# Cross-attention on one core: row sums by a transposing VectorE pass, a turned slot order, and variances from ScalarE

## The reference

```python
Q, K, V = split_heads(x @ Wq + bq), split_heads(ctx @ Wk + bk), split_heads(ctx @ Wv + bv)
scores = einsum('bhqd,bhkd->bhqk', Q, K) / sqrt(32)
attn = softmax(scores, axis=-1)                      # over 77 keys
out = merge_heads(einsum('bhqk,bhkd->bhqd', attn, V)) @ Wo + bo
y = out + x
mu, var = mean(y), mean(square(y - mu))              # over the 512 features
result = (y - mu) * rsqrt(var + 1e-5) * gamma + beta
```

## Time and profile before

| | |
|---|---|
| median of 3 runs | 676.41 us (676.19 to 676.54) |
| the profiled execution | 677.69 us, its span 675.9 us |
| mean granted TensorE clock | 0.983 |
| busy TensorE, VectorE, GpSimd, ScalarE | 643.8, 555.0, 453.7, 319.7 us |
| chain of waits, by engine | TensorE 77%, VectorE 6%, SP's queue 6% |

### The profile page before, as it was taken

How to read it: one execution, slowest core, us unless ns; L and a number is a source line. 1 busy time by engine, 2 the same in 40 slices (tenths; PEclk the granted TensorE clock), 3 DMA queues, 4 the chain that set the end, 5 groups by cost and what they waited for, 6 DMA issues and landing times.

```text
span 675.9 us, 11503 instructions
## 1 busy us (share of the span) xinstructions
PE 643.8 (95%) x3336; PEld 435.1 (64%) x3336; DVE 555.0 (82%) x842; ACT 319.7 (47%) x547; POOL 453.7 (67%) x396
## 2 busy tenths in 40 slices
PE   6989997999999999999999999999999999999990
PEld 5978754666666666666666666666666666665570
DVE  5534484888889898888988888889888888988986
ACT  5612254545545555554555545455554544544431
POOL 0422143477777777777787777777877777666897
PEclk9999996999999999999999999999999999999996
DMA  9757788767776868778787778686767778675512
GB/s 318 288 198 186 193 203 208 179 162 199 194 201 170 209 180 205 204 195 215 201 197 184 201 186 204 190 201 186 198 177 206 198 205 215 152 185 154 162 62 93
DMA packets 105677, 129.55 MB, mean 192 GB/s; under 512 B 49936, under 2 KB 49936, under 8 KB 105648
## 3 DMA queue, kind: packets, MB, share of 16 engines
q1 hardware_dynamic: 105648, 129.19, 71.8%
HBM read 53.94 MB, written 24.35 MB: 116 GB/s over the span
## 4 chain that ended last, share of the span: by engine, by line
PE 77%; DVE 6%; SPq 6%; issue 2%; POOL 1%; DMA 1%; ACT 0%; POOLq 0%; DVEq 0%; ACTq 0%
PE p_q L584 24%; PE p_o L646 23%; PE p_s L614 9%; PE p_v L627 9%; PE p_d L630 7%; PE p_a L600 5%; SPq L519 3%; DVE rden L799 2%; SPq L505 1%; DMA xt<-in_x_t 1%; DVE cxt L813 1%; DVE stats L795 1%; DVE y L793 0%; POOL rstd L932 0%; DVE stats L887 0%
## 5 line engine op out<-in xcount | busy, mean ns | idle before, releaser
L799 DVE RECIPROCAL rden<-p_d 128x512 f32<-128x512 f32 x64 | 214.9, 3358 | 27.8 <-PE p_d L630 27.7
L709 ACT ACTIVATE prob<-p_s 77x512 f32<-77x512 f32 x256 | 144.0, 588 | 111.4 <-PE p_s L614 111.0
L834 DVE TENSOR_REDUCE nm<-p_a 128x4 f32<-128x308 f32 x256 | 117.4, 462 | 29.3 <-PE p_a L600 26.0
L936 POOL TENSOR_TENSOR y<-y,gamma_row 128x512 f32<-128x512 f32 x60 | 76.7, 1278 | 70.7 <-ACT y L739 70.7
L926 POOL TENSOR_TENSOR xl<-xt,xh 128x512 fp32r<-128x512 f32 x60 | 77.5, 1291 | 64.8 <-ACT xh L716 63.5
L584 PE MATMUL p_q<-xh,wqh 128*128 128x512 f32 x256 | 101.8, 398 | 1.7 <-PEq L148 1.7
L584 PE MATMUL p_q<-xl,wqh 128*128 128x512 f32 x256 | 101.8, 398 | 0.0
L584 PE MATMUL p_q<-xh,wql 128*128 128x512 f32 x256 | 101.1, 395 | 0.0
L945 POOL TENSOR_TENSOR cl<-cxt,ch 128x512 fp32r<-128x512 f32 x64 | 82.5, 1288 | 26.3 <-ACT ch L734 26.3
L739 ACT ACTIVATE y<-y,nmr,rstd 128x512 f32<-128x512 f32 x60 | 48.9, 815 | 106.1 <-DVE nmr L818 106.1
L614 PE MATMUL p_s<-z,ks 97*77 97x512 f32 x256 | 95.7, 414 | 0.0
(11 more groups left out here) (114 smaller groups left out, 911.8 us busy)
## 6 DMA issues: line engine op xcount, KB each, us to landing
z<-qh SPq DMA_DIRECT2D x256, 128.0 KB, 2.7
xt<-in_x_t SPq DMA_DIRECT2D x64, 256.0 KB, 2.8
z<-ql SPq DMA_DIRECT2D x128, 128.0 KB, 2.4
xn<-in_x SPq DMA_DIRECT2D x60, 256.0 KB, 3.1
out_dram<-y SPq DMA_DIRECT2D x60, 256.0 KB, 3.3
ks<-k_high SPq DMA_DIRECT2D x32, 154.0 KB, 3.5
cx<-in_ctx_t SPq DMA_DIRECT2D x4, 616.0 KB, 5.4
k_high<-kth SPq DMA_DIRECT2D x4, 616.0 KB, 3.5
```

Source lines behind the costliest of these rows:

```text
L709: nc.scalar.activation(prob[0:S2, j, :], p_s[j % 2][0:S2, :], ACT.Exp, scale=SCALE).then_inc(prob_ready, 1)
L799: nc.vector.reciprocal(rden[:], p_d[:]).then_inc(rden_ready, 1)
L834: nc.vector.tensor_reduce(nm[:, t, HC * (g.k % 2):HC * (g.k % 2 + 1)], p_a[t % 2][:, 0:HC * S2].rearrange("p (h k) -> p h k", k=S2), AX_X, ...
```

## The change: what it does

The sums over keys are formed in two steps. VectorE's new `sum_keys` reduces `prob` (96 partitions, rows from 64 on zeroed once at the start and then written as far as 77) with a transposing `tensor_reduce`: each block of 32 x 32 is turned and summed, which leaves `part`, 96 x 64. TensorE adds the three blocks of 32 with a 0/1 matrix `sel` into 16 columns per head (`p_den`); `invert_sums` takes the reciprocal of 16 columns and spreads it to `rden` with a transposition.

`add_residual` now yields the row sums as well (`accum_out`); a small operation makes the negated mean, ScalarE's new `square` yields the sum of squared deviations (its elementwise output goes to `xn`, unused), and `variance_of_squares` replaces `bn_stats` and `bn_aggr` for all but the last four tiles.

The slots are turned: maxima in the chunk's own slot, scores at + 2, values at + 3, out projection at + 7, norm at + 8, store at + 10. TensorE's slot begins with all of p_q. SP issues the z copies in the odd slot of the pair itself and the maxima in the next slot. The program has 67 slots instead of 69. The V products that are left to `attend` move up (`V_SLOTS`), and so does the loading of `Wo` (`WO_SLOTS`).

```diff
+KP = 3 * DK
...
-LAG_ROWMAX = 1
-LAG_PV = 5
-LAG_SCORE = 4
-LAG_OUT = 9
-LAG_NORM = 10
-LAG_SCALE = 11
-LAG_STORE = 12
+LAG_SCORE = 2
+LAG_PV = 3
+LAG_OUT = 7
+LAG_NORM = 8
+LAG_SCALE = 9
+LAG_STORE = 10
+WO_SLOTS = (3, 5)
 
 V_FIRST = 4
-V_SLOTS = (0, 1, 1, 2, 3, 3)
+V_SLOTS = (0, 0, 1, 1, 2, 2)
...
-                nc.gpsimd.memset(keep["ones"][:], 1.0)
                 nc.gpsimd.memset(keep["minus_half"][:], -0.5)
+                sel = keep["sel"]
+                nc.gpsimd.memset(sel[:], 0.0).then_inc(sel_ready, 1)
+                for b in range(KP // DK):
+                    pool.wait_ge(sel_ready, b + 1)
+                    nc.gpsimd.affine_select(out=sel[:], in_=sel[:], compare_op=ALU.not_equal, fill=1.0, base=-DK * b,
+                                            pattern=[[-1, DK]], channel_multiplier=1).then_inc(sel_ready, 1)
...
             def slot(g):
-                if g.k % 2 == 1 and g.back(3).valid(NG):
-                    load_maxima(g.back(3))
                 if g.k % 2 == 0 and g.back(2).valid(NG):
-
-
-                    c = g.back(2)
+                    load_maxima(g.back(2))
+                if g.k % 2 == 1 and g.back(1).valid(NG):
+
+
+                    c = g.back(1)
                     i = c.k // 2 % 2
                     all_at_least(sp, (qh_ready, c.over(1, 2)), (ql_ready, c.over(1, 2)),
                                  (s_summed, c.over(2, -1, HALF)))
@@ -518,14 +530,14 @@
                         for j in range(HC):
                             sp.dma_start(z[DK * part:DK * (part + 1), i, j::HC, :].bitcast(F32),
                                          src[DK * j:DK * (j + 1), i, :, :].bitcast(F32)).then_inc(z_in[i], 16)
-                if g.k % NCH == 1 and g.valid(NG):
-                    load_ks(g.back(1))
-                if g.k % NCH == 3 and g.valid(NG):
-                    load_v(g.back(3))
-                if g.k % NCH == NCH - 1 and g.back(-1).valid(NG):
-                    if g.back(NCH - 1).is_first():
+                if g.k % NCH == 0 and g.valid(NG):
+                    load_ks(g)
+                if g.k % NCH == 2 and g.valid(NG):
+                    load_v(g.back(2))
+                if g.k % NCH == 1 and g.back(1 - NCH).valid(NG):
+                    if g.back(1).is_first():
                         sp.wait_ge(kb1_zeroed, 1)
-                    load_kb(g.back(-1))
+                    load_kb(g.back(1 - NCH))
...
-                    all_at_least(sp, (y_ready, m.over(1, -1)))
+                    all_at_least(sp, (squared, m.over(1, -1)))
                     sp.dma_start(xn[:, m.k % 2, :], x_dram[m.over(1)]).then_inc(xn_in[m.k % 2], 16)
...
+                pe.wait_ge(part_ready, g.over(1, 1))
+                at_least(pe, rec_ready, g.over(1))
                 for j in range(HC):
-                    last = nc.tensor.matmul(p_d[DK * j:DK * (j + 1), :], ones[0:S2, :], prob[0:S2, j, :],
+                    last = nc.tensor.matmul(p_den[DK * j:DK * (j + 1), 0:QB], sel[:], part[:, QB * j:QB * (j + 1)],
                                             start=True, stop=True)
...
-                q, r, s, v, o = g, g.back(LAG_ROWMAX), g.back(LAG_SCORE), g.back(LAG_PV), g.back(LAG_OUT)
+                s, v, o = g.back(LAG_SCORE), g.back(LAG_PV), g.back(LAG_OUT)
+                if g.valid(NG):
+                    for kc in range(KC):
+                        project_q(g, kc)
                 if v.valid(NG):
                     values(v)
                 if s.valid(NG):
                     scores(s, 0)
                     scores(s, 1)
-
-
-                parts = [(project_q, q, kc) for kc in range(KC) if q.valid(NG)]
-                parts += [(project_out, o, kc) for kc in range(KC) if o.valid(NS)]
-                if len(parts) == 2 * KC:
-                    scores_after, maxima_after = (1, 3), (2, 4, 5, 6)
-                elif s.valid(NG):
-                    scores_after, maxima_after = (0, 1), (1, 2, 3, 3)
-                else:
-                    scores_after, maxima_after = (), (0, 1, 2, 3)
-                for n, (project, chunk, kc) in enumerate(parts):
-                    project(chunk, kc)
-                    for j, after in enumerate(scores_after):
-                        if s.valid(NG) and after == n:
-                            scores(s, 2 + j)
-                    for t, after in enumerate(maxima_after):
-                        if r.valid(NG) and after == n:
-                            rowmax_scores(r, t)
+                for kc in range(KC):
+                    if o.valid(NS):
+                        project_out(o, kc)
+                    if s.valid(NG) and kc in (1, 2):
+                        scores(s, kc + 1)
+                    if g.valid(NG):
+                        rowmax_scores(g, kc)
...
                     at_least(act, pv_summed, g.over(1))
+                    at_least(act, part_ready, g.over(1))
...
+            def square(m):
+
+                i = m.k % 4
+                act.wait_ge(nmean_ready, m.over(1, 1))
+                nc.scalar.activation(xn[:, m.k % 2, :], y[:, i, :], ACT.Square, bias=nmean[:, i, :],
+                                     accum_out=ssd[:, i, :]).then_inc(squared, 1)
...
-                short = is_short(g)
-                if s.valid(NG):
-                    exp(s, 0)
-                    exp(s, 1)
                 if n.valid(NG):
                     split_x_high(n)
-                if s.valid(NG):
-                    exp(s, 2)
-                if s.valid(NG) and short:
-                    exp(s, 3)
                 if g.valid(NG):
                     q_high(g)
-                if s.valid(NG) and not short:
-                    exp(s, 3)
+                if m.valid(NS):
+                    square(m)
+                if s.valid(NG):
+                    for j in range(HC):
+                        exp(s, j)
                 if v.valid(NG):
                     ctx_high(v)
...
+            nc.vector.memset(prob[DK * 2:KP, :, :], 0.0).then_inc(const_dve, 1)
...
-                nc.vector.tensor_tensor(y[:, i, :], p_o[:], xn[:, m.k % 2, :], ALU.add).then_inc(y_ready, 1)
+                nc.vector.scalar_tensor_tensor(out=y[:, i, :], in0=p_o[:], scalar=0.0, in1=xn[:, m.k % 2, :],
+                                               op0=ALU.add, op1=ALU.add,
+                                               accum_out=ysum[:, i, :]).then_inc(y_ready, 1)
                 dve.wait_ge(y_ready, m.over(1, 1))
-                nc.vector.bn_stats(stats[:, i, :], y[:, i, :]).then_inc(stats_ready, 1)
+                nc.vector.tensor_scalar(nmean[:, i, :], ysum[:, i, :], -1.0 / D, None,
+                                        ALU.mult).then_inc(nmean_ready, 1)
+
+            def sum_keys(g):
+
+                dve.wait_ge(prob_ready, g.over(1, 1, HC))
+                at_least(dve, pv_summed, g.over(1))
+                nc.vector.tensor_reduce(part[:], prob[0:KP, :, :].rearrange("p h (i r) -> p (h i) r", r=DK),
+                                        AX_X, ALU.add, apply_transpose=True).then_inc(part_ready, 1)
 
             def invert_sums(g):
+
                 dve.wait_ge(pv_summed, g.over(1, 1))
-                nc.vector.reciprocal(rden[:], p_d[:]).then_inc(rden_ready, 1)
+                at_least(dve, rden_ready, g.over(1))
+                nc.vector.reciprocal(rec[:], p_den[:, 0:QB]).then_inc(rec_ready, 1)
+                dve.wait_ge(rec_ready, g.over(1, 1))
+                at_least(dve, cx_ready, g.over(1))
+                nc.vector.transpose(rden[:].rearrange("p (i r) -> p i r", r=DK),
+                                    rec[:].unsqueeze(2).broadcast_to([P, QB, DK])).then_inc(rden_ready, 1)
...
+            def variance_of_squares(m):
+
+                i = m.k % 4
+                dve.wait_ge(squared, m.over(1, 1))
+                nc.vector.tensor_scalar(ve[:, i, :], ssd[:, i, :], 1.0 / D, EPS, ALU.mult, ALU.add).then_inc(ve_ready, 1)
+
+            def minus_mean_over_std(m):
+                i = m.k % 4
+                dve.wait_ge(rstd_ready, m.over(1, 1))
+                nc.vector.tensor_tensor(nmr[:, i, :], nmean[:, i, :], rstd[:, i, :], ALU.mult).then_inc(nmr_ready, 1)
...
-                r, v, m = g.back(LAG_ROWMAX), g.back(LAG_PV), g.back(LAG_NORM)
+                v, m = g.back(LAG_PV), g.back(LAG_NORM)
+                if v.valid(NG):
+                    sum_keys(v)
                 if m.valid(NS):
                     add_residual(m)
-                    dve.wait_ge(stats_ready, m.over(1, 1))
+                if g.valid(NG):
+                    q_low(g)
                 if v.valid(NG):
                     invert_sums(v)
-                spread = not g.back(LAG_OUT).valid(NS)
-                for t in range(2 if spread else 1):
-                    if r.valid(NG):
-                        row_maxima(r, t)
-                if v.valid(NG):
                     divide(v)
                 if m.valid(NS):
-                    variance(m)
```

(59 more changed lines are left out.)

15 lines of the change are left out of this document (8 added, 7 removed).

## The result

The changed kernel takes 966.79 us (median of 4 runs, 961.56 to 971.32), the kernel before beside it 676.47 (676.19 to 676.96): ratio 1.429 (95% interval 1.421 to 1.436). Its profiled span is 966.4.

The account below looks back on a forecast made before the run. TensorE at full clock bounds the kernel before; after the change, a loop through SyncE's queue. Pair 3 starts at 146, 28 rounds (25.6 or 27.7) take 744, to 890, and the end 50: 940 us, range 846 to 1008.

Parts of the forecast that it names:

- z start to the scores: From a pair's first z issue, through SyncE's queue, to the landing of its maxima: 13.8 us, later with kb.
- rest of TensorE's slot, clock included: TensorE's scores, out groups and maxima products in slot g+1: 4.4 us, plus 2.5 lost to half clock after the wait.
- to q_low and SP: Slot g+2 from p_q to the end of q_low, with the handover to SyncE's queue: 4.9 us.
- round: One pass of the closed loop, two slots, from z issues to next z issues: 25.6 us, or 27.7 with kb.
- the term of 2.0: Landing time of the last maxima copy, counted from the start of its issue in SyncE's queue: 2.0 us.
- The rival with the clock up: The loop binds but TensorE's clock stays at full rate after the waits: 862 us, chance 0.18.
- step 4: Slot g+2 to q_low: TensorE's path 4.6 us, VectorE's list with nmr and sum_keys 4.8; 4.9 taken with handover.
- the ring: Closed loop: z issues, maxima, scores, rest of TensorE's slot, next q_low, next z issues; predicted to set the time.
- The rival with two passes: VectorE's transposing reduction passes its elements twice, 2.1 us more a round: 1005 us; chance 0.13 shared with a slower clock return.
- TensorE's waits: TensorE idle before p_s in 32 even slots: 6 us each, 8 with kb, some 200 us in all.
- the tail: From pair 31's z start to the kernel's end: its scores, three short slots, last layernorm and store; 50 us.
- The rival of a kernel at 617: The loop doesn't bind and TensorE's smaller work shows: 36 us less in full slots, 23 at the end; chance 0.04.

Follow-up runs that it names:

- f4: The changed kernel with only the small product nmr written as tensor_scalar instead of tensor_tensor; 929.4 us, ratio 1.373.
- e2: The changed kernel with all arithmetic kept and only the lags two slots larger, as before the change; 941.34 us, ratio 1.390.
- h1: The changed kernel with lags one slot larger, xt and xn loads first, nmr as tensor_scalar, old V_SLOTS, kb issues one slot later behind the maxima; 646.81 us, ratio 0.956.
- e4: The changed kernel with four of the twelve z copies per pair issued by ScalarE's queue instead of SyncE's; 910.57 us, ratio 1.345.
- e5: The changed kernel with 30 or 18 extra, resultless 128x512 products on TensorE before the first scores of each even slot; 935.93 us, ratio 1.382.

## Why the prediction was right

The time, 966.79, lies 27 above the 940 predicted, and the mechanism was the one named. Term by term, on a round without kb (421.05 to 447.28) and one with it (393.15 to 421.05). The second row ends here with the last maxima product, some 0.24 later than the start of p_q taken above:

| term | predicted | without kb | with kb |
|---|---|---|---|
| z start to the scores | 13.8 / 15.9 | 13.84 | 16.40 |
| rest of TensorE's slot, clock included | 4.4 + 2.5 | 7.15 | 6.25 |
| to q_low and SP | 4.9 | 5.24 | 5.25 |
| round | 25.6 / 27.7 | 26.23 | 27.90 |

- *The issues and the landing.* 13.8 was right without kb. With kb it was 0.5 short: kb's issues and what lies between took 2.4 and not 2.1. From the start of the last issue of the maxima to the scores, the term of 2.0, it took 1.9 to 2.1 in each round from pair 4 to pair 30.
- *The clock.* The half rate came back in each round as forecast, with 2.75 and 1.85 for 2.5, and 2.3 on the mean. The rival with the clock up (862) fell. That the loss came so near 2.5 is in part luck: the two rows behind it gave only bounds of 0 and 4.5. The Trainium skill (TensorE: Matmul & The Clock Gate, "HAM oscillation — how this bites in real kernels") states the same return to half rate at each wait, and the trace agrees: 0.50 granted behind waits of 6.6 and 9.1 us.
- *VectorE's list.* The sum of step 4 was 0.35 short, and one of its terms is the worst miss of all: nmr was put at 0.2, "the fixed part", and takes 0.86 on the mean and 1.1 in these rounds. The others took less in the chain (part 2.22 of 2.28, the residual 0.6 of 0.74, the mean 0.06 of 0.2), which hid it. I read a duration as a property of the operation; what runs beside it on GpSimd is part of the price, and f4 gives that price, 37 us. Of it 31 x 0.9 = 28 is the direct part, one nmr a round in the ring at 1.1 for 0.19. In the means of the rounds it is the third stretch, 4.57 for 5.47. The other 9 stand in the second, TensorE's behind the first scores, which takes 6.15 for 6.59; the granted clock of the whole run is 0.836 for 0.820, but why it comes back sooner was not shown.
- *The prices that no row showed.* The transposing reduction 2295 ns for 2.28 us; four products of 16 columns 0.25 a slot for 0.2; the reciprocal 0.248 for 0.25; the square 0.718 for 0.7 to 0.8 (the rows named for it, hold VectorE's passes and none of ScalarE's; the size was right all the same). The rival with two passes fell by this.
- *TensorE's waits.* 6 and 8 us, 200 in all, was too low: 249.8, or 7.8 each. The last releaser is the maxima's landing in 161.0 of it; the rest the trace puts down to the issue.
- *The sum.* Pair 3 starts at 149.65 for 146 (+3.7, of which 2.9 stand before the first z copies, 66.85 for 64); 28 rounds take 758.0 for 744 (27.07 a round for 26.6; +14); the tail 58.7 for 50 (+8.7). Together 26.4, the whole miss. Of the tail, 2.6 come before the last scores: the loads of the last row tiles (xt, vb, bv_row and a longer xn: 2.3 us of issues from 915.46 on) stand in SP's queue there, so that the maxima start 11.05 behind the z start for 9.6 in the round above, and the scores start 3.1 behind the last of them, not 2.0, for which the trace names no cause. 3.6 come in the three short slots, the first at half clock, and in the next VectorE stands 2.45 before nmr until the inverse root comes. 2.7 come behind the last division, where nmr takes 1.23 and 1.15. I had left the loads of the last tiles out of the queue, the very thing that decides.

Where the argument was incomplete: it named one ring and said that the slack of more than a slot between z and scores was what the change took away. e2 gives the slack back and gains 25 of 290. The queue closes three rings, through z and the maxima, through xt and through xn, and each is hidden behind the one before. The prediction had looked at xn and said only that it is issued long after the square; it did not ask who waits for xn. This didn't touch the time, since the first ring is the longest, but it would have misled anybody who wanted to mend the kernel. The rival of a kernel at 617 fell. With all rings loosened h1 comes to 646.81, and where it stays above 617 can be read from the z starts: from pair 3 to pair 31 it takes 471.6 for 507.5 before, so 36 less, the very 36 that the rival assumed. But pair 3 starts 12.2 later (121.2 for 109.0), and of the 23 assumed at the end 4.8 came (54.6 for 59.4).

## What to carry to other kernels

Before moving an issue in an in-order queue, write down for each transfer in it who needs it first and how late it may come; a wait in front of twelve issues delays all that stand behind, also those that need nothing from it. Loads that wait for nothing belong ahead of copies that wait. When one ring is longest, a cure of it moves the time only down to the next: undo singly and together before a part is called innocent. A tiny operation can cost as much as what its neighbour engine is doing.

## What of the hardware was not expected

- A VectorE product of 128x1 with two SBUF tensors took 864 ns on the mean beside GpSimd's passes, 190 as tensor_scalar, and the kernel as a whole 37 us.
- Issues from two queues slow each other: 0.85 and 0.79 us each in e4, where 0.65 and 0.63 are usual.
- The granted clock fell to 0.57 in a stretch behind only 2.17 us without work, although 18 dense products stood ahead (e5).
- The transposing reduction costs 2295 ns for 2048 elements, the same 1.0 ns an element over some 0.2 us as bn_stats of 512 (694 ns); ScalarE's read of its accumulator 187 ns, VectorE's 75.
